# Hybrid attention block on one core: the narrow context of attention A in four whole-chunk parts instead of six

## What is computed

```python
x = x + attn_a(layernorm(x))   # 16 heads of 64: q = softmax over d, k = softmax over tokens,
                               # context = q^T k per head, out = context @ v, then w_out and b_out
x = x + ffn(layernorm(x))      # sigmoid gate * (relu(k)^2 @ W_v), inputs mixed with the token before
x = x + attn_b(layernorm(x))   # 16 heads of 8, rotary positions, softmax over 512 x 512 scores
x = x + ffn(layernorm(x))
```

## Time and profile before

| | |
|---|---|
| median of 3 runs | 983.1 us (982.38, 983.1, 985.3) |
| profiled execution, its own time | 981.95 us |
| its span, first to last instruction | 980.1 us |
| outside the span | 1.85 us |
| busy: PE, DVE, ACT, POOL | 896.1, 712.2, 673.9, 597.7 us |
| mean granted TensorE clock | 0.972 of full speed |
| chain that ended last, by engine | PE 55%, DVE 22%, issue 8%, ACT 7%, POOL 5% |
| instructions on PE / DVE | 9743 matmul records / 1494 |

### The profile page before, as it was taken

How to read it: one execution, slowest core, us unless ns; L and a number is a source line. 1 busy time by engine, 2 the same in 40 slices (tenths; PEclk the granted TensorE clock), 3 DMA queues, 4 the chain that set the end, 5 groups by cost and what they waited for, 6 DMA issues and landing times.

```text
span 980.1 us, 24338 instructions
## 1 busy us (share of the span) xinstructions
PE 896.1 (91%) x9743; PEld 533.3 (54%) x9743; DVE 712.2 (73%) x1494; ACT 673.9 (69%) x657; POOL 597.7 (61%) x425
## 2 busy tenths in 40 slices
PE   5988889898989989999999999999999999889884
PEld 3767545555555555656565565655556655333332
DVE  4777646879887787888878787879888686754234
ACT  4565658585767767777777777777777777677860
POOL 3757376675775668676757687785768566445100
PEclk9999889999999999999999999999999999999995
DMA  5012142324233232333333242423342332323310
GB/s 169 23 34 87 44 141 88 101 67 125 64 101 99 77 108 65 117 101 88 109 99 108 77 127 66 130 69 111 96 130 66 96 100 76 109 65 108 87 33 15
DMA packets 68684, 87.63 MB, mean 89 GB/s; under 512 B 13649, under 2 KB 40146, under 8 KB 68562
## 3 DMA queue, kind: packets, MB, share of 16 engines
q1 hardware_dynamic: 68562, 85.96, 29.5%
HBM read 16.19 MB, written 20.97 MB: 38 GB/s over the span
## 4 chain that ended last, share of the span: by engine, by line
PE 55%; DVE 22%; issue 8%; ACT 7%; POOL 5%; SPq 2%; DMA 1%; DVEq 0%; ACTq 0%; POOLq 0%
PE PS L1741 15%; PE PS L1697 7%; PE PS L1604 5%; PE PS L1536 4%; PE PS L1538 4%; PE PS L1537 4%; DVE q_sum L1023 3%; PE PS L1650 3%; PE PS L1657 3%; DVE cT L1201 3%; POOL work L495 3%; PE PS L1531 3%; DVE mom L966 3%; ACT work L760 2%; DVE cT L1203 2%
## 5 line engine op out<-in xcount | busy, mean ns | idle before, releaser
L760 ACT ACTIVATE work<-PS 128x2048 f32<-128x2048 f32 x150 | 282.1, 1881 | 129.2 <-PE PS L1697 129.2
L760 ACT ACTIVATE work_b<-PS 128x2048 f32<-128x2048 f32 x74 | 139.2, 1881 | 66.9 <-PE PS L1697 66.9
L1741 PE MATMUL PS<-work,v 128*32 128x512 f32 x1368 | 177.8, 613 | 0.5 <-ACT work L767 0.5
L750 ACT ACTIVATE work<-PS 128x512 f32<-128x512 f32 x256 | 148.7, 596 | 32.0 <-PE PS L1538 29.1
L482 POOL TENSOR_TENSOR rs<-ve,half_neg 128x4 f32<-128x4 f32 x64 | 68.0, 1062 | 156.4 <-DVE ve L972 156.0
L495 POOL TENSOR_TENSOR work<-work,q_rcp 128x1024 f32<-128x1024 f32 x64 | 125.2, 1956 | 43.7 <-DVE q_rcp L1026 43.7
L1536 PE MATMUL PS<-wqk,h1h 128*128 128x512 f32 x256 | 126.1, 492 | 15.3 <-DVE qkv_sb L1100 12.5
L1697 PE MATMUL PS<-q_st,k_st 32*128 32x512 f32 x896 | 115.8, 506 | 12.6 <-issue 4.3
L1538 PE MATMUL PS<-wqk,h1l 128*128 128x512 f32 x256 | 103.3, 403 | 0.0
L1537 PE MATMUL PS<-wqk,h1h 128*128 128x512 f32 x256 | 103.0, 402 | 0.0
L508 POOL TENSOR_TENSOR mask_cos<-qkv_sb,cos_t 128x1024 f32<-128x1024 f32 x16 | 38.1, 2379 | 94.3 <-DVE qkv_sb L1100 93.0
(11 more groups left out here) (181 smaller groups left out, 1746.9 us busy)
## 6 DMA issues: line engine op xcount, KB each, us to landing
qkv_scratch<-qkv_sb SPq DMA_DIRECT2D x16, 768.0 KB, 4.6
rot<-qkv_sb SPq DMA_DIRECT2D x32, 256.0 KB, 3.2
k_st<-qk_hi SPq DMA_DIRECT2D x128, 64.0 KB, 2.1
q_st<-qk_hi SPq DMA_DIRECT2D x128, 64.0 KB, 2.1
k_st<-qk_lo SPq DMA_DIRECT2D x128, 64.0 KB, 2.1
q_st<-qk_lo SPq DMA_DIRECT2D x128, 64.0 KB, 2.1
parted<-U SPq DMA_DIRECT2D x52, 128.0 KB, 2.9
xa<-in_attn_a_x SPq DMA_DIRECT2D x16, 256.0 KB, 3.1
```

The lines of the kernel that those rows point to most:

```text
L750: act.activation((EQ, EK)[r // 2][c % 2][:, (r % 2) * 512:(r % 2) * 512 + 512], PS[:, bank, :], ACT.Exp)\
L760: act.activation(probs_of(z, b, n), PS[:, 0:4, :], ACT.Exp).then_inc(z["s_exp"].sem, 1)
L1741: mm = pe.matmul(PS[32 * h:32 * h + 32, 6, :], v_flat[p][:, kc, at:at + 32], probs_of(z, b, n)[:, h, :], start=(n % 8 == 0), stop=(n % 8 = ...
```

## The change

Chunk 1's context moves whole to pair k = 5 and chunk 2's whole to k = 7. The parts in k = 4 and k = 6 go, with their waits, and so do the waits for `c_sum` ahead of halves 9 and 13. VectorE has one add per chunk of 512 elements a row in place of two of 256: `c_add` after `sums_of(a, 2)`, after `sums_of(a, 3)`, and at the start of the next step. `c_sum` counts four in a step and not six. The diff is whole:

```diff
--- before.py
+++ after.py
@@ -208,7 +208,7 @@
         ph_mm, ph_exp = sig("ph_mm", 16), sig("ph_exp", 16)
         q_rc, q_hat, c_mm, c_ev = sig("q_rc", 2 * NC), sig("q_hat", NC), sig("c_mm", 2 * NC), sig("c_ev", 3)
 
-        c_sum = Since(sig("c_sum", 6), 2)
+        c_sum = Since(sig("c_sum", NC), 2)
         t_mm, m_mm, m_ev, y_mm, xb_ok, x1_ok = (sig(s) for s in ("t_mm", "m_mm", "m_ev", "y_mm", "xb_ok", "x1_ok"))
         t_ev = sig("t_ev", 2)
 
@@ -1027,20 +1027,18 @@
 
             def c_add(i, n):
 
-                pairs = (range(0, 8), range(0, 4), range(4, 8), range(0, 4), range(4, 8), range(0, 8))[n]
-                part = PS[:, 5, :].rearrange("p (a n) -> p a n", a=PAIRS)[:, pairs[0]:pairs[-1] + 1, :]
-                at = ctx_sum[:, pairs[0]:pairs[-1] + 1, :]
-                hold(dve, c_mm, i, (2, 3, 4, 5, 6, 8)[n])
+                part = PS[:, 5, :].rearrange("p (a n) -> p a n", a=PAIRS)
+                hold(dve, c_mm, i, 2 * n + 2)
                 if n == 0:
-                    dve.tensor_copy(at, part).then_inc(c_sum.sem, 1)
+                    dve.tensor_copy(ctx_sum, part).then_inc(c_sum.sem, 1)
                 else:
                     hold(dve, c_sum, i, n)
-                    dve.tensor_tensor(at, part, at, ALU.add).then_inc(c_sum.sem, 1)
+                    dve.tensor_tensor(ctx_sum, part, ctx_sum, ALU.add).then_inc(c_sum.sem, 1)
 
             def c_copy(i):
 
                 hold(dve, c_mm, i)
-                dve.tensor_copy(ctx_sum, PS[:, 5, :].rearrange("p (a n) -> p a n", a=PAIRS)).then_inc(c_sum.sem, 6)
+                dve.tensor_copy(ctx_sum, PS[:, 5, :].rearrange("p (a n) -> p a n", a=PAIRS)).then_inc(c_sum.sem, NC)
 
             def c_totals(i, src):
                 dve.reduce_sum(z_sum[:, :], src, AX_X).then_inc(c_ev.sem, 1)
@@ -1309,7 +1307,7 @@
                 if E:
                     split_h3(l)
                     pv_copy(z, e, 1)
-                    c_add(s, 5)
+                    c_add(s, 3)
                     hold(dve, c_sum, s)
                     c_totals(s, ctx_sum)
                     qkv_free(l)
@@ -1352,8 +1350,6 @@
                 if not E:
                     p_copy(l, 2)
                 scale_and_mix(f1, s)
-                if A:
-                    c_add(a, 1)
                 pv_copy(z, b, 0)
                 if E:
                     x3_stats(z, 3, e)
@@ -1361,22 +1357,20 @@
                 relu(f1, s, other)
                 if A:
                     sums_of(a, 2)
-                    c_add(a, 2)
+                    c_add(a, 1)
                 gate_v(f1, s, other)
                 add_x2(s)
                 if E:
                     scale_and_mix(f2, e)
                 elif there(a + 1):
                     h1_copy(a + 1, 1 - p)
-                if A:
-                    c_add(a, 3)
                 x2_stats(s)
                 if E:
                     hold(dve, f1["act"], s)
                     relu(f2, e, other)
                 if A:
                     sums_of(a, 3)
-                    c_add(a, 4)
+                    c_add(a, 2)
                 if E:
                     gate_v(f2, e, other)
                     hold(dve, z["out_st"], e - 1)
@@ -1862,18 +1856,12 @@
                     if k == 3 and A:
                         hold(pe, ph_exp, a, 6)
                         context_narrow(a, 0)
-                    if k == 4 and A:
-                        hold(pe, ph_exp, a, 8)
-                        context_narrow(a, 1, range(0, 4))
                     if k == 5 and A:
                         hold(pe, ph_exp, a, 10)
-                        context_narrow(a, 1, range(4, 8))
-                    if k == 6 and A:
-                        hold(pe, ph_exp, a, 12)
-                        context_narrow(a, 2, range(0, 4))
+                        context_narrow(a, 1)
                     if k == 7 and A:
                         hold(pe, ph_exp, a, 14)
-                        context_narrow(a, 2, range(4, 8))
+                        context_narrow(a, 2)
                     scores(z, b, 2 * k + 1)
 
 
@@ -1946,7 +1934,6 @@
                             hold(pe, z["x3_ok"], e)
                         ffn_k(f1, s, other)
                         if A:
-                            hold(pe, c_sum, a, 2)
                             proj_half(a, p, 9, False)
                             hold(pe, ph_exp, a, 9)
                         ffn_r(f1, s, None, 4 if A else 7)
@@ -1955,7 +1942,7 @@
                         if A:
                             hold(pe, f1["gate"], s)
                             proj_half(a, p, 10, False)
-                            hold(pe, c_sum, a, 3)
+                            hold(pe, c_sum, a, 2)
                             proj_half(a, p, 11, False)
                             hold(pe, f1["x"], s, 1)
                         else:
@@ -1974,7 +1961,6 @@
                                 hold(pe, f1["x"], s, 1)
                             ffn_k(f2, e, other)
                         if A:
-                            hold(pe, c_sum, a, 4)
                             proj_half(a, p, 13, False)
                         if E:
                             if A:
@@ -1987,7 +1973,7 @@
                             if E:
                                 hold(pe, f2["gate"], e)
                             proj_half(a, p, 14, False)
-                            hold(pe, c_sum, a, 5)
+                            hold(pe, c_sum, a, 3)
                             proj_half(a, p, 15, False)
                         if E and A:
                             hold(pe, f2["x"], e, 1)
```

## The result

The changed kernel takes 996.88 us, the median of four runs (992.19 to 1004.47). The kernel before, run beside it, takes 983.37 (982.38 to 985.3). The ratio is 1.0147, with an interval from 1.0115 to 1.0179; by the medians it is 13.5 us slower. The profiled execution took 998.34 us, 996.6 of it span. The direction and the range of the prediction hold, its 1,012.0 us is 15 too much.

What follows compares the result with a forecast made beforehand. It took TensorE's queue plus its holes to bound the kernel. 981.95 + 27.9 for seven more long steps + 1.7 in-step gave 1011.6, 1012.7 against the median; it said 1012.0 us, range 983 to 1017, likeliest case 1006 to 1017.

Steps and rivals of the forecast that it cites:

- What bounds the kernel and why a step is long: TensorE's queue and holes; steps 4 to 7 are 3.99 us longer each, by a VectorE and GpSimd race at the statistics.
- Why the packet comes early or late: TensorE's instruction count times the 16 KB load; the change makes 1,286 a step 1,282, so drift falls from six to two.
- The margin at step 14: Step 14's load would be 22 instructions ahead of step 3's, two less than the 24 still late at step 7.
- no packet 1.5 to 3.5 us after S2: Sign of being right: no instruction-loading packet in that window after a step's third score group.
- The price of a packet: The skill calls the cost of crossing an instruction block mostly hidden; by that the prediction's large term would be nil.
- all of steps 4 to 14 should have it late, `rot` early, and VectorE stuck: 7 x 3.99 = +27.9: Late instruction packets in steps 4 to 14 would make seven more long steps, 8 to 14: +27.9 us.
- no DMA is moved, and SP's and GpSimd's orders stand: Within a step, transfers and the orders of SP's and GpSimd's queues were taken as unchanged by the edit.
- I count 0: VectorE's five context instructions becoming three, with longer merged adds, cost 0; -0.3 us a step as the other end.
- In-step sum, +0.14: Score gaps of pairs five to eight: 0.44 + 0.44 - 0.55 - 0.19 = +0.14 us a step, +1.7 over steps 4 to 15.
- Rival 1: Only 2 to 6 of steps 8 to 14 turn long: 8 to 24 us, 992 to 1009; chance 0.12.
- rival 2: The race stays as it is, since the count does not fix the load's time: 982 to 986; chance 0.17.
- rival 3: Faster: moved blocks cost nothing in the sixth and eighth pairs, -8.9 us, 973 to 974; chance 0.12.

Runs made afterwards that it cites:

- Experiment 1: The kernel before, with GpSimd's multiply by the sines made to wait for VectorE's statistics of the next batch's first norm: 963.52 us, ratio 0.9813.
- experiment 4: The kernel before with four redundant TensorE waits a step taken out, 1,282 instructions a step, computation and order unchanged: 1006.6 us, ratio 1.0224.
- experiment 5: The changed kernel with GpSimd's bias add held until VectorE's output add of the step before is done: 1013.41 us, ratio 1.0306.
- experiment 3: The changed kernel with four satisfied waits a step put back on TensorE, 1,286 instructions a step again: 984.05 us, ratio 0.9995.
- experiment 9: The kernel before with 16 further instructions of satisfied waits ahead of TensorE's first work, steps unchanged: 976.44 us, ratio 0.9912.
- experiment 10: The kernel before with 40 further instructions of satisfied waits ahead of TensorE's first work, steps unchanged: 972.76 us, ratio 0.9864.
- experiment 2: The changed kernel with GpSimd's multiply by the sines made to wait for VectorE's statistics of the next batch: 971.14 us, ratio 0.9865.
- the changed one with both waits: The changed kernel with GpSimd's multiply by the sines held behind VectorE's statistics and its bias add behind the output add: 963.02 us, ratio 0.9803.

## Why the prediction was right and wrong

- **What bounds the kernel and why a step is long**: right. Experiment 1 takes the collision away and the four long steps go; experiments 4 and 5 make it in eleven. The sum took the 3.99 us of a long step whole and so had the clock's part in it without naming it.
- **Why the packet comes early or late**: right, and now shown. TensorE has 451 semaphore instructions at L188 in place of 503, four fewer in each of 13 steps. Experiments 3, 4, 9 and 10 move the packet by the count. The margin at step 14 was larger than I knew: the edge lies between 28 and 30. But "no packet 1.5 to 3.5 us after S2", which I had named as a sign of being right, failed in four of eleven steps (4, 8, 12 and 14, at 3.2 to 3.5 us). What decides is its distance to the issue of `rot`, which the prediction held fixed.
- **The price of a packet**: the Trainium skill (Runtime: NRT & Kernel Launch, Instruction fetch mechanics) calls the cost of crossing a block mostly hidden. In experiment 4 four instructions a step fewer made 22.6 us; they came through the transfer that the packet meets, of which the sentence says nothing.
- **The step that failed** is "all of steps 4 to 14 should have it late, `rot` early, and VectorE stuck: 7 x 3.99 = +27.9". The packet did come later than before in each of steps 8 to 14 (3.2 to 4.1 us after S2, against 1.9 to 3.3), but `rot` was early in two of them only. I let only the packet move and left `rot` where it was, issued from 1.1 us after S2 at the latest, because "no DMA is moved, and SP's and GpSimd's orders stand". The orders stood; the times did not. Two of seven steps became long, 9.9 us in place of 27.9. With the delay taken away (experiment 5) there are all seven, and 1,013.4 us.
- **Why `rot` moved**: the sentence on VectorE, "I count 0" for what its instructions do at the end of a step, has the hole. It counted their lengths with nothing beside them. The output add runs beside GpSimd's bias add, and ends 0.55 us after it. At step 12 that is 0.41 us after the step's first score group in the changed kernel (618.71 and 618.30), and with it in the kernel before (608.74 and 608.73), and the store, `k_st`, `q_st`, `parted` and `rot` hang on it in SyncE's queue. GpSimd's order stood here too, and its times did not: L482, which waits for VectorE's statistic L972, starts 7.89 us ahead of that score group in the kernel before (600.84) and 7.48 in the changed one (610.82), and the bias add behind it is nearer by the same 0.41. Why L972 comes later is not shown. The earlier trace rows held the other half: a transfer is later by where the packet falls, and the same kind of packet falls into the issues too.
- **In-step sum, +0.14**: the gaps came out as forecast (2.55, 3.18, 2.55, 3.18), in every step from 4 on. What the short steps lost beyond it, 0.5 to 0.8 us each, is in experiment 2's gap: in step 12 of the kernel before the multiply of `cT` took 1.36 us, in that of the changed kernel 2.58, and TensorE waits for what is behind it.
- **Rival 1** is what happened, in outcome: two to six more long steps, 992 to 1,009. Its reason (the margin at the end, or a count that isn't four) is not: the two are steps 10 and 14, with short ones between and the packet later than before in all. It had a chance of 0.12. So the time lies in the stated range, but outside 1,006 to 1,017, the forecast's own, and that the range took it in is no merit of the mechanism: its lower part was there for rival 2. Rivals 2 and 3 fell with the packet's times and the gaps.

Of VectorE's 14.7 us of further busy time, 13.3 are in steps 8 to 14. Three instructions with two operands in SBUF have most of it, here by the sum of a line: the kernel before, the changed one, and the changed one with both waits. After the bar stand the busy time in us and the mean in ns:

```profile
L1120 DVE SCALAR_TENSOR_TENSOR x<-gated,x 128x512 f32<-128x512 f32 x7 | 8.3, 1185 | 1.1 <-DVE gated L1115 0.5
...
L1120 DVE SCALAR_TENSOR_TENSOR out_sb<-gated,x 128x512 f32<-128x512 f32 x7 | 5.8, 824 | 0.7
...
L1203 DVE TENSOR_TENSOR cT<-parted,cT 128x512 f32<-128x512 f32 x7 | 12.5, 1779 | 0.2
```

```profile
L1118 DVE SCALAR_TENSOR_TENSOR x<-gated,x 128x512 f32<-128x512 f32 x7 | 14.4, 2051 | 0.7
...
L1118 DVE SCALAR_TENSOR_TENSOR out_sb<-gated,x 128x512 f32<-128x512 f32 x8 | 9.5, 1188 | 0.8
...
L1201 DVE TENSOR_TENSOR cT<-parted,cT 128x512 f32<-128x512 f32 x7 | 14.1, 2017 | 0.2
```

```profile
L1122 DVE SCALAR_TENSOR_TENSOR x<-gated,x 128x512 f32<-128x512 f32 x7 | 15.0, 2143 | 0.7
...
L1205 DVE TENSOR_TENSOR cT<-parted,cT 128x512 f32<-128x512 f32 x7 | 10.6, 1508 | 0.2
...
L1122 DVE SCALAR_TENSOR_TENSOR out_sb<-gated,x 128x512 f32<-128x512 f32 x7 | 4.8, 693 | 0.7
```

The first add has 14.4 - 8.3 = 6.1 us of it and costs no time of its own, for it is as long in the last kernel, at 15.0. The output add has 1,188 ns against 824 and 693, the multiply 2,017 against 1,779 and 1,508, which is 2.5 and 1.7 us over seven steps. The small statistics instructions have 5.9 us more, from the two further long steps, and the merged context adds 2.2 less.

What stays open: why the packet holds one issue for 0.7 us in one step and for 2.2 in another, and why the output add is not late in step 14's start; with these, why just 10 and 14 are the long ones. Also open is what a smaller collision of the same kind costs that all these kernels still have: L966, on 128x4 elements, takes 1.87 us in each of steps 4 to 14 while GpSimd's L495 runs (344.06 and 343.99 in step 7 of the kernel before). The runs of the changed kernel spread over 12 us (992 to 1,004), and three long steps more or fewer are 12 us; that they are such steps was not seen, for there is one profile.

## What to carry to other kernels

When steps that do the same work fall into two lengths, look for two engines that race for one thing, and order them with an explicit wait: here one wait on GpSimd was worth 20 us, more than the edit it was to judge cost, and with a second one the kernels of 1,282 and 1,286 instructions a step came out alike (with the first alone they stood 7.6 us apart). Until that is done, a small edit can't be judged on such a kernel: four waits a step more or fewer were worth 13 and 23 us here, the edit itself nothing that could be measured. And when a term says "this transfer goes as before", check the issue of it, back through its queue, to the instruction that starts the queue's step, and what runs beside that instruction.

## What was not expected of the hardware

- When a 16 KB packet of instruction loading comes, the DMA issue on SyncE that is under way or the one after it lasts 0.7 to 2.2 us instead of 0.6, and ends 0.2 to 0.4 us after the packet. No run shows why.
- A VectorE instruction with two operands in SBUF that overlaps a two-operand instruction of GpSimd which started first, by as little as 0.07 us, ends 0.54 to 0.56 us after the latter ends, for 128x512 elements: 0.55 (L1118, ahead of step 12), 0.56 (L1201), 0.54 (experiment 2), and 0.55 for the second multiply of `cT` in all the short steps 4 to 14 of both kernels. Its alone-time is 0.69 us. GpSimd was not longer for it (L517 2.37). Where VectorE's output add started 0.2 us first (steps 5 to 8, 11 and 15 of the kernel before), it was GpSimd's bias add that took longer, 1.73 us instead of 1.30. The Trainium skill (SBUF — State Buffer, Who interferes with whom) has such an instruction and a GpSimd instruction that reads SBUF take turns, the later one blocked until the earlier ends; these rows agree, and add the 0.55 us that are left to do after it. The prediction had met such a collision at L968 and not looked for one at the output add.
- Satisfied waits have a price or a yield by their place in the count alone: 16 of these instructions before the first work, -8.9 us; four a step taken out, +22.6.
- The 3.1 us that TensorE waits in a long step are followed, in all ten long steps of the two kernels, by a stretch with a granted clock of 0.50; by the estimates above it costs 0.6 to 1.1 us. In two steps of experiment 10 the same wait stands without such a stretch.
